# Conditioned residual kernel: half of the stores moved from ScalarE's DMA queue to GpSimd's

## The reference

```python
x = x + einsum('bct,bcd->bdt', x, W0[itok_B_0_15])
x = x + einsum('bct,bcd->bdt', x, W1[itok_B_0_31]) + bias1[itok_B_0_31] (over t)
```

## Time and profile before

| | |
|---|---|
| Median of three executions | 642.38 us |
| The profiled execution | 642.87 us |
| its span | 641.1 us |
| TensorE busy | 537.6 us (84%) |
| VectorE busy | 329.2 us (51%) |
| ScalarE busy | 333.2 us (52%) |
| GpSimd busy | 123.9 us (19%) |
| Moved by the DMA engines | 271.82 MB, 424 GB/s over the span |
| Load, median from issue to landing | 27.0 us |
| Store, median from issue to landing | 40.5 us |

### The profile page before, as it was taken

How to read it: one execution, slowest core, us unless ns; L and a number is a source line. 1 busy time by engine, 2 the same in 40 slices (tenths; PEclk the granted TensorE clock), 3 DMA queues, 4 the chain that set the end, 5 groups by cost and what they waited for, 6 DMA issues and landing times.

```text
span 641.1 us, 6225 instructions
## 1 busy us (share of the span) xinstructions
PE 537.6 (84%) x2308; PEld 234.0 (37%) x2308; DVE 329.2 (51%) x259; ACT 333.2 (52%) x385; POOL 123.9 (19%) x263
## 2 busy tenths in 40 slices
PE   1899999999889888898898888988988988889870
PEld 0344444443334333343333333333433433334330
DVE  0366666665455445545554555455445544554460
ACT  0466666666455455554554555556545555555450
POOL 2222222222121121221221212212212112122000
PEclk9999999999999999999999999999999999999995
DMA  9999999999999999999999999999999999999995
GB/s 359 428 414 430 428 432 429 429 430 432 431 429 432 431 430 431 431 430 431 430 431 431 430 429 432 430 433 429 431 433 428 429 433 430 429 432 430 430 429 255
DMA packets 18931, 271.82 MB, mean 424 GB/s; under 512 B 2241, under 2 KB 2274, under 8 KB 2274
## 3 DMA queue, kind: packets, MB, share of 16 engines
q1 hardware_dynamic: 9504, 137.37, 50.4%
q10 hardware_dynamic: 9410, 134.26, 49.0%
HBM read 137.40 MB, written 134.22 MB: 424 GB/s over the span
## 4 chain that ended last, share of the span: by engine, by line
DMA 73%; PE 20%; DVE 3%; POOLq 0%; issue 0%; ACT 0%; DVEq 0%; POOL 0%; SPq 0%; ACTq 0%
DMA out_dram<-xt 42%; DMA xt<-in_x_dram 30%; PE acc L160 17%; PE acc L155 3%; DVE xt L224 2%; DMA w_sb<-in_w_dram 1%; DVE xt L226 1%; DVEq L39 0%; ACT L246 0%; POOLq L127 0%; POOLq L130 0%; POOL map0T L137 0%; POOL map L138 0%; ACT both L247 0%; ACT both L246 0%
## 5 line engine op out<-in xcount | busy, mean ns | idle before, releaser
L160 PE MATMUL acc<-xt,both 64*128 64x512 f32 x2048 | 471.7, 602 | 70.6 <-DMA xt<-in_x_dram 68.2
L251 ACT ACTIVATE xt<-acc,bias_of 64x1024 f32<-64x1024 f32 x256 | 283.6, 1108 | 272.3 <-PE acc L160 269.9
L224 DVE TENSOR_SCALAR xt<-acc,bias_of 64x1024 f32<-64x1024 f32 x128 | 163.3, 1276 | 279.8 <-PE acc L160 279.8
L160 PEld LDWEIGHTS acc<-xt,both 64*128 64x128 f32 x2048 | 189.5, 187 | 321.5 <-issue 224.1
L226 DVE TENSOR_SCALAR xt<-acc,bias_of 64x1024 f32<-64x1024 f32 x128 | 165.0, 1289 | 1.9
L137 POOL TENSOR_TENSOR map0T<-w0T_sb,ident 128x128 f32<-128x128 f32 x128 | 65.4, 511 | 467.8 <-PE acc L155 456.1
L155 PE MATMUL acc<-map,map0T 128*128 128x256 f32 x256 | 73.3, 409 | 0.9 <-POOL map L138 0.9
L138 POOL TENSOR_TENSOR map<-w_sb,ident 128x128 f32<-128x128 f32 x128 | 65.3, 510 | 0.0
L155 PEld LDWEIGHTS acc<-map,map0T 128*128 128x128 f32 x256 | 43.8, 191 | 52.3 <-issue 47.8
L247 ACT ACTIVATE both<-acc 64x256 f32<-64x256 f32 x64 | 24.2, 378 | 0.7
L246 ACT ACTIVATE both<-acc 64x256 f32<-64x256 f32 x64 | 24.1, 377 | 0.7
(11 more groups left out here) (4 smaller groups left out, 0.4 us busy)
## 6 DMA issues: line engine op xcount, KB each, us to landing
xt<-in_x_dram SPq DMA_DIRECT2D x64, 2048.0 KB, 27.0
out_dram<-xt ACTq DMA_DIRECT2D x64, 2048.0 KB, 40.5
w_sb<-in_w_dram SPq DMA_DIRECT2D x1, 2048.0 KB, 9.3
w0T_sb<-in_w0T_dram SPq DMA_DIRECT2D x1, 1024.0 KB, 4.8
cond_sb<-in_conds_dram ACTq DMA_DIRECT2D x1, 1.0 KB
bias_sb<-in_bias_dram ACTq DMA_DIRECT2D x1, 16.0 KB, 9.4
cond_rep<-in_conds_dram ACTq DMA_DIRECT2D x1, 16.0 KB, 11.1
```

The costliest lines, as they stand in the source:

```text
L160: return nc.tensor.matmul(acc[:, j * CHUNK:(j + 1) * CHUNK], both[k * HC:(k + 1) * HC, buf, u, :], xt[k * HC:(k + 1) * HC, slot, u * T + j ...
L224: nc.vector.tensor_scalar(xt[0:HC, q % SLOTS, a:a + HALF], acc0[0:HC, a:a + HALF], bias_of[0:HC, 2 * q:2 * q + 1], None, ALU.add)
L251: return nc.scalar.activation(xt[HC:C, q % SLOTS, v * T + a:v * T + a + HALF], acc1[v * HC:(v + 1) * HC, a:a + HALF], ACT.Identity, bias=b ...
```

## The change

The stores of odd pairs are issued by GpSimd, those of even pairs still by ScalarE. GpSimd has the store of pair q - 3 in its program behind the maps of pair q (q even, from 4 on), and the last two odd stores, of pairs 61 and 63, behind all maps. Each engine waits at the end for the slots that it stored.

```diff
+            def store(q):
+                pool.wait_ge(hi_out0, q + 1)
+                pool.wait_ge(hi_out1, q + 1)
+                pool.dma_start(out_pairs[q, :, :], xt[:, q % SLOTS, :]).then_inc(stored[q % SLOTS], LOAD)
+
             for b in range(B):
...
                 nc.gpsimd.tensor_tensor(map1[:, q % 2, k, :, :], w1_v[:, bass.ds(i1[b % GROUP], 1), :, :], ident_v,
                                         ALU.add).then_inc(maps_ready, 1)
+                if k == 1 and q >= 3 and q % 2 == 0:
+                    store(q - 3)
+            for q in range(PAIRS - 3, PAIRS):
+                if q % 2 == 1:
+                    store(q)
+            for q in range(1, SLOTS, 2):
+                pool.wait_ge(stored[q], LOAD * TURNS)
...
                 odd_out(q, 1, HALF).then_inc(hi_out1, 1)
-                act.wait_ge(hi_out0, q + 1)
-                act.wait_ge(hi_out1, q + 1)
-                act.dma_start(out_pairs[q, :, :], xt[:, q % SLOTS, :]).then_inc(stored[q % SLOTS], LOAD)
-            for q in range(SLOTS):
+                if q % 2 == 0:
+                    act.wait_ge(hi_out0, q + 1)
+                    act.wait_ge(hi_out1, q + 1)
+                    act.dma_start(out_pairs[q, :, :], xt[:, q % SLOTS, :]).then_inc(stored[q % SLOTS], LOAD)
+            for q in range(0, SLOTS, 2):
                 act.wait_ge(stored[q], LOAD * TURNS)
```

## The result

The changed kernel takes 651.75 us (median of six executions, 650.41 to 654.41) against 642.51 us for the kernel before on the same chip: a ratio of 1.0149, interval 1.0133 to 1.0166. It is 9.2 us slower. The forecast had the sign and the exposed end of the run right, but 4.7 us for the size; 651.75 lies above its range of 644.3 to 650.7. The profiled execution took 654.34 us with a span of 652.5, so it is one of the slower of the six, and sums over its rows come out at 11.4 us and not at 9.2.

The account below looks back on a forecast made before the run. The prediction took the DMA engines, at 431 GB/s, as the bound. It added 4.7 us of idle time at the end, including 0.5 for GpSimd's issue, to 642.38: 647.1 us, range 644.3 to 650.7.

Parts of the forecast that it names:

- What bounds the kernel: Whole run: the DMA engines are the bound at 431 GB/s, 9.7 us a pair; only their idle time matters.
- Issue: GpSimd issuing 32 stores: covered by its waits in the steady state; only the last store's 0.5 us on the path.
- Span 641.1 + 4.7: Whole run: span before plus 4.7 us of idle time at the end gives 645.8 us.
- The bound of the step, 4.1 us at most for the last store: GpSimd's issue of the last store: 4.1 instead of 0.5 us, 3.6 more, taking the range to 650.7 us.
- Shares: Queues served in turn: stores get 2/3 while both store queues work; store about 16 us, load 51, no store backlog.
- The finer point on GpSimd's packets: GpSimd's stores: if packets held all eight rows of an engine, odd stores pass loads almost at once; 649.7 us, not 647.1.
- In the steady state no gain and no loss: Middle of the run: engines stay full at 431 GB/s with five loads outstanding, so no time changes.
- The end: After the last load lands: 17.6 us needed, 12.3 us of work, 0.6 behind the last data, so 4.7 us idle.
- It has no pause elsewhere: Last DMA engine: same work and no other pause, so the whole run ends 4.7 us later.
- the price for each start of a queue: Rival, each store's start: 0.8 us lost, 26 to 51 us in all, 668 to 693 us; chance 0.12 above 650.7.
- The lag of the last engine: Rival "Faster", end of run: 2.5 to 5 us of the last engine's lag come back, 637 to 641.1 us; chance 0.08.
- nothing would have changed: Rival, whole run: engines full whoever issues, store backlog stays; 642.4 us, 641.6 to 643.6; chance 0.20.

Follow-up runs that it names:

- The mirror with two load queues: Kernel before with odd pairs loaded by GpSimd, even ones by SyncE, all stores by ScalarE: 643.93 us against 642.44.

## Why the prediction was right about the end of the run and short in its size

**What bounds the kernel: right.** With two queues, whatever left the engines full until the end (all stores by GpSimd, less its drain; only the last one; the kernel before with the last pair uncomputed) stayed at 642.5.

**Issue: the step that failed, by what it left out.** The prediction costed GpSimd's stores at their issue, 0.5 us for the last one, and the issue itself was right: its instruction takes 0.57 us, maps were never late, and with one store moved nothing changed. But a store by GpSimd has a second part at the end of the program, some 83 ns for each one issued, in the drain. With 32 stores and a store of GpSimd as the last of all, 2.7 us stand on the path. The prediction's sum "Span 641.1 + 4.7" left the time behind the last landing at the 0.5 us of before; it became 3.2. No row of the kernel before had a drain behind GpSimd's transfers. The bound of the step, 4.1 us at most for the last store, would have covered it, but it was put to the issue, and the value taken came from the wrong thing. With these 2.7 us the forecast would have been 649.8, still inside its range; the steady state, below, has most of the rest.

**Shares: right.** Store 15 to 16 us, load 50. The mirror with two load queues and the run with GpSimd in the first half only both behaved as equal turns say. The waits for loads begin earlier, as forecast: at pair 10 where it was pair 16 (forecast: about 9). What was not forecast is their form: they became fewer and longer, 38 of up to 6.1 us against 48 of up to 1.5.

```profile
PE acc L172 <- DMA xt<-in_x_dram: 69.1, 38, 6.1
```

The finer point on GpSimd's packets also went the way of the sum. By the Trainium skill, DMA: Bandwidth & Descriptors, Queues, rings and completion order, a packet of many descriptors is drained before the turn passes on; had all eight rows of an engine been one packet, GpSimd's stores would have been much faster than ScalarE's. They took 16.3 us against 15.4, so the trace does not show such packets for rows of 16 KB.

**"In the steady state no gain and no loss": the second step that failed, a term put at nothing, wrong by 1 to 1.5 us.** The windows of 100 to 600 us give 431 GB/s with two queues, 427 to 429 with three throughout, and the rate comes back to 431 in the half of a run that has two again. The runs in which neither the end nor the drain is exposed put 1.5 us (three queues throughout, on the load side) and 1.1 us (first half only) on it. In the profiled executions of the changed kernel, both slower than the median, it is more: 429 and 427 GB/s instead of 431 over 500 us are 2.3 and 4.6 us.

What goes with it can be read from the 16 counts of each load. In the kernel before, a load's first and last count are 5.2 us apart (median of the loads that land from 350 to 600 us), with all stores by GpSimd 5.7. In the changed kernel they are 23.1 us apart, 18.0 in its second profiled execution, and those of a store only 1.7 and 1.8. With the third queue on the load side it is the stores that are spread, over 10.9 us, and the loads' 2.1. So the 16 engines come apart in the queue that holds the long backlog. A slot is free for the next step only when its slowest engine has landed; that the engines ahead of it run short of work meanwhile, and that this is the lost rate, is argued and not shown. The granted clock of TensorE is lower in the same stretches (0.95 against 1.00 in the rows above); no run separates the two. But when stores were held back in the second half of the run with two queues, the clock was 1.00 from 350 to 600 us and the rate 429, so the clock alone does not make it.

**The end: right in its size, too simple in its picture.** Forecast were 4.7 us of idle time, with GpSimd's 0.5 in it. Taking the last computation away gave back 4.2 to 5.1 us in the changed kernel, and nothing in the kernel before. But the forecast had the engines full until the last load lands, and gaps only behind it. The rate fell from 610 us on: the engines that were some 20 us ahead had finished their loads by then, and at 628 to 630 us the loads' queue moved two packets of 16 KB. "It has no pause elsewhere" is said of the last engine alone, and for that one it is not shown either way; for the others it is wrong.

Against the forecast's own terms, the profiled execution has the last load at 632.7 and not 627.7 (5.0 more), 16.6 us from there to the last landing and not 17.6 (1.0 less), and the 2.7 us behind it: 6.7 us over the forecast of 4.7. The second profiled execution has 631.4 for the last load. The 1.5 us that the lower clock added there to the last products show that TensorE's time is back on the path once the end is exposed, which may be a part of why the changed kernel's six executions differ by 4.0 us and those of the kernel before beside them by 0.7.

The sum as measured: end 4.2 to 5.1, drain and the last issue 2.95 (of which 0.5 were in the forecast), middle 1 to 1.5. That is 8.2 to 9.5 against 9.2; each term is a difference of medians and can be off by a microsecond or more.

Of the rivals, the price for each start of a queue, at 26 us and above, did not come: 429 GB/s instead of 431 over the 50 stores from 100 to 600 us is 0.05 us each, not 0.8. The lag of the last engine gave nothing back that any run shows. By the rule of the Trainium skill, DMA: Bandwidth & Descriptors, Rules for kernel authors, that spreading DMAs over issuing engines only saves issue time, nothing would have changed; the runs show that the division among queues decides what is queued at the end, which that rule does not speak of.

None of these kernels beats the one before; the nearest ones equal it.

## What to carry to other kernels

In a kernel like this one, bound by DMA and with its buffers reused in a ring, the queues' turns decide how the ring is divided between loads and stores, and a backlog of stores at the end is what hides the last computation. A third queue on the store side eats that backlog, though the rate in the middle hardly shows it; so look at what is outstanding when the last load lands, and whether all 16 engines are equally far. With two queues, stores by GpSimd cost nothing on the way, but their drain belongs into the sum if one of them is among the last to land.

## What the runs showed of the hardware that was not expected

- GpSimd's drain, where it starts behind the landing of its last store, takes 82 to 84 ns more for each store of 2 MB that it issued: 0.14 us after 1, 2.60 after 31, 2.68 after 32, 5.29 after 64. Whether it goes by stores, packets or bytes was not varied.
- With two queues the rate is 431 GB/s whether ScalarE or GpSimd issues the stores; with three it is 427 to 429, and within one run it returns to 431 when the third queue stops.
- In the changed kernel the 16 counts of one load of 2 MB are spread over 23.1 and 18.0 us (median of 350 to 600 us, two executions) where they are spread over 5.2 in the kernel before.
- With TensorE's waits of up to 1.5 us the granted clock of 100 to 600 us stayed at 1.00; with waits of up to 6.1 us it is 0.96 in the same window of the changed kernel. After some of the longer waits 16 matmuls took 5.40 us and not 3.70, with a granted clock of 0.68 over those 5.40 us, so a part of them at the lower of its two levels, 1.2 GHz. In the middle of the run, where the DMA engines are the bound, no run puts a price on it; at the exposed end it cost 1.5 us in one profiled execution.

```profile
604.79 5.40 PE L172 MATMUL acc<-xt,both 64*128 64x512 f32 x16 [1.94 <-DMA xt<-in_x_dram]
...
627.44 3.70 PE L172 MATMUL acc<-xt,both 64*128 64x512 f32 x16
```
